# Attention phase: the next image's token sums made during the current image's output part, head sums ahead of four projection units, flows in another PSUM bank

## What is computed

```python
qkv = x @ W_qkv.T
q, k, v = (to_heads(part) for part in split(qkv))
q, k = sigmoid(q), sigmoid(k)
k_sum, q_sum = k.sum(axis=2), q.sum(axis=2)
sink_incoming   = 1 / (((q + EPS) * (k_sum + EPS)).sum(-1) + EPS)
source_outgoing = 1 / (((k + EPS) * (q_sum + EPS)).sum(-1) + EPS)
conserved_sink   = ((q + EPS) * ((k * source_outgoing).sum(2) + EPS)).sum(-1) + EPS
conserved_source = clip(((k + EPS) * ((q * sink_incoming).sum(2) + EPS)).sum(-1) + EPS, -1, 1)
kv  = einsum(k, v * softmax(conserved_source) * n)
out = einsum(q, kv) * sink_incoming * sigmoid(conserved_sink)
t   = t + out @ W_proj.T + b_proj
```

## Time and profile before

| | before |
|---|---|
| median of 3 executions | 5605.55 us (5603.51 to 5610.34) |
| profiled execution, its own time | 5614.06 us |
| its span in the profile | 5612.2 us |
| attention phase in the span | about 4040 to 5165 us |
| first head sums of image 0, of image 7 | start at 4094.8 us, at 5031.9 us |
| TensorE / VectorE / GpSimd busy over the span | 94% / 70% / 44% |
| mean granted TensorE clock over the span | 0.968 of full speed |

### The profile page before, as it was taken

The page is one execution under the profiler, slowest core; times in us unless marked ns, Lnnn a source line. Parts: engine busy times, 40 slices in busy tenths (PEclk is TensorE's granted clock), DMA queues, the critical chain, the costliest instruction groups (busy, mean ns, idle before and its releaser), DMA issues. The chain is left out here.

```text
span 5612.2 us, 90234 instructions
## 1 busy us (share of the span) xinstructions
PE 5297.2 (94%) x26964; PEld 3688.4 (66%) x26964; DVE 3942.1 (70%) x6109; ACT 2461.5 (44%) x4685; POOL 2495.2 (44%) x1385
## 2 busy tenths in 40 slices
PE   8999869998999999999998999999799999987999
PEld 5667545554555555555556777777676666665999
DVE  4555556665899999999995666676545555555787
ACT  4444238786334343443333555555532222210555
POOL 0000024442899999999995555555201111111332
PEclk9999879999999999999999999999899999997999
DMA  1111568887444444444446666666523333322443
GB/s 44 39 52 40 139 165 245 242 243 219 143 149 151 151 148 152 147 151 150 149 135 188 208 209 213 206 217 204 163 86 101 102 97 104 102 82 82 120 123 113
DMA packets 364270, 810.15 MB, mean 144 GB/s; under 512 B 45135, under 2 KB 149507, under 8 KB 354618
## 3 DMA queue, kind: packets, MB, share of 16 engines
q1 hardware_dynamic: 341648, 731.51, 44.3%
q10 hardware_dynamic: 22512, 77.20, 3.6%
HBM read 448.08 MB, written 360.49 MB: 144 GB/s over the span
## 5 line engine op out<-in xcount | busy, mean ns | idle before, releaser
L717 POOL TENSOR_TENSOR co_prod<-co_cross 111x512 f32<-111x512 f32 x448 | 850.2, 1898 | 0.0
L651 ACT ACTIVATE co_y_out<-co_y_ps 112x512 f32<-112x512 f32 x448 | 267.9, 598 | 927.6 <-PE co_y_ps L597 922.8
L714 POOL TENSOR_TENSOR co_prod<-co_direct 111x512 f32<-111x512 f32 x448 | 577.4, 1289 | 202.1 <-PE co_y_ps L597 115.4
L691 DVE TENSOR_TENSOR co_direct<-co_v_ps,co_spec 111x1024 f32<-111x1024 f32 x448 | 543.3, 1213 | 92.3 <-PE co_v_ps L135 87.8
L1917 POOL TENSOR_TENSOR at_t<-at_t,at_p_bias 112x1024 f32<-112x1024 f32 x56 | 134.2, 2409 | 976.1 <-DMA at_t<-t_tiles 976.1
L693 DVE TENSOR_TENSOR co_cross<-co_v_ps,co_spec 111x1024 f32<-111x1024 f32 x448 | 541.3, 1208 | 0.0
L135 PE MATMUL co_v_ps<-co_v_high,co_col_fwd_high 112*111 112x512 f32 x896 | 506.1, 565 | 1.4 <-DVE co_cross L693 1.4
L595 PE MATMUL co_y_ps<-co_prod,co_col_inv 111*112 111x512 f32 x896 | 458.2, 592 | 0.0
L597 PE MATMUL co_y_ps<-co_prod,co_col_inv 111*112 111x512 f32 x896 | 457.5, 592 | 0.1
L671 DVE TENSOR_TENSOR co_v_low<-co_v_in,co_v_high 112x1024 fp32r<-112x1024 f32 x224 | 372.4, 1662 | 0.1
L2081 ACT ACTIVATE at_qk_t<-at_bank_ps 128x448 f32<-128x448 f32 x224 | 121.8, 544 | 567.9 <-PE at_bank_ps L135 567.8
(11 more groups left out here) (267 smaller groups left out, 14107.8 us busy)
## 6 DMA issues: line engine op xcount, KB each, us to landing
v_rows<-pr_rows_out SPq DMA_DIRECT2D x56, 1792.0 KB
co_v_in<-v_rows SPq DMA_DIRECT2D x448, 224.0 KB
y_rows<-co_y_out SPq DMA_DIRECT2D x448, 224.0 KB
mx_y_in<-y_rows SPq DMA_DIRECT2D x224, 448.0 KB, 5.5
kern_rows<-kr_rows_out SPq DMA_DIRECT2D x28, 896.0 KB
st_x_in<-x SPq DMA_DIRECT2D x56, 448.0 KB, 11.4
pr_x_in<-x SPq DMA_DIRECT2D x112, 224.0 KB
mx_x_in<-x SPq DMA_DIRECT2D x56, 448.0 KB, 4.8
```

The source lines that it names most:

```text
L651: nc.scalar.activation(y_out[:, b, :], y_ps[b % 2][:2 * SIDE, :], ACT.Copy).then_inc(y_ready, 1)
L691: nc.vector.tensor_tensor(direct[b % 2][:], v_ps[b % 2][:POINTS, :], spec[i][:, :2 * WIDE], ALU.mult).then_inc(real_terms, 1)
L714: nc.gpsimd.tensor_tensor(prod[b % 2][:, :WIDE], direct[b % 2][:, :WIDE], direct[b % 2][:, WIDE:], ALU.subtract).then_inc(real_ready, 1)
L717: nc.gpsimd.tensor_tensor(prod[b % 2][:, WIDE:], cross[b % 2][:, :WIDE], cross[b % 2][:, WIDE:], ALU.add).then_inc(combined, 1)
```

## The change

VectorE: the token sums become a function `sum_tokens(im)`. For the first image it runs before the loop. For every other image it runs in the output part of the image before, at step j = 6, between `add_residual(5)` and `measure(5)`. TensorE: the head sums stand at the head of `back`, and units 0 to 3 stand behind them. The first flows go to bank 6 in place of bank 2. Before the gram part, `turn_keys(0)` and `turn_keys(1)` stand ahead of the `z` matmuls; unit 18 moves from before `add_gram(0)` to behind n = 1, and unit 19 from behind n = 4 to behind n = 5. The wait for `t2_ready` ahead of the first head sums stays. Nothing is added to or taken from the computation.

```diff
-        flow_ps = kept_ps = z_ps = kv_out_ps = bank[2]
+        flow_ps = bank[6]
+        kept_ps = z_ps = kv_out_ps = bank[2]
...
-                    units(0)
                     pe.wait_ge(t2_ready, b * SUMS)
                     pe.wait_ge(upd_ready, b * UPDS)
                     wait_link(pe, im, "sel")
                     head_sums(total_eps, flow_ps, flow_mm)
-                    units(1, 2, 3)
+                    units(0, 1, 2, 3)
                     wait_link(pe, im, "inv_low")
...
                     last.then_inc(turn_mm, 1)
+                    turn_keys(0)
+                    turn_keys(1)
                     for h in range(HALVES):
                         last = nc.tensor.matmul(z_ps[:, h:h + 1], z_rows[:, h, :], z_part[:], start=True, stop=True)
                     last.then_inc(z_mm, 1)
-                    turn_keys(0)
-                    turn_keys(1)
-                    units(18)
                     for n in range(NT):
                         add_gram(n)
                         if n + 2 < NT:
                             turn_keys(n + 2)
-                        if n == TILES:
-                            units(19)
+                        if n in (1, TILES + 1):
+                            units(18 + n // TILES)
...
+                def sum_tokens(im):
+
+                    dve.wait_ge(qt_ready, (im.b + 1) * UNITS)
                     step("total", nc.vector.reduce_sum(total[:], part[im.odd][:], axis=AX.X))
                     wait_link(dve, im, "total")
                     step("total_eps", nc.vector.tensor_scalar(total_eps[:], total[:], ATT_EPS, None, ALU.add))
                     wait_link(dve, im, "total_eps")
                     select("sel", total_eps)
...
                         if j:
                             add_residual(j - 1)
+                            if front and j == CHUNKS - 1:
+                                sum_tokens(ahead)
                             measure(j - 1)
...
                 low_part(first.after(), 1)
+                sum_tokens(first)
                 over_images(dve, back)
```

More of the change, by code:

```diff
@@ L2153, in low_part, with step, select @@
                     nc.vector.tensor_tensor(low[:], n_raw[im.slot(i)][:], high[:].bitcast(F32), ALU.subtract).then_inc(low_ready, 1)
+                def step(name, instruction):
+                    instruction.then_inc(link, 1)
+                mask3 = head_mask.unsqueeze(1).to_broadcast([128, 2, HB])
+                def select(name, sums):
+                    for x in (0, 2):
+                        y = (x + 2) % BLOCKS
+                        last = nc.vector.tensor_tensor(sel_heads[:, x:x + 2, :], mask3,
+                                                       sums[:, y:y + 2].unsqueeze(2).to_broadcast([128, 2, HB]), ALU.mult)
+                    step(name, last)
+                def sum_tokens(im):
+                    dve.wait_ge(qt_ready, (im.b + 1) * UNITS)
+                    step("total", nc.vector.reduce_sum(total[:], part[im.odd][:], axis=AX.X))
+                    wait_link(dve, im, "total")
+                    step("total_eps", nc.vector.tensor_scalar(total_eps[:], total[:], ATT_EPS, None, ALU.add))
+                    wait_link(dve, im, "total_eps")
+                    select("sel", total_eps)
                 def back(im, front, beyond):
@@ L2160, in next_low @@
                             low_part(ahead, i)
-                    def step(name, instruction):
-                        instruction.then_inc(link, 1)
                     def split_rows(name, values):
@@ L2169, in split_rows @@
                         step(name + "_low", nc.vector.tensor_tensor(rows[1][:], values[:], rows[0][:].bitcast(F32), ALU.subtract))
[L2171 to L2186, removed]
                     dve.wait_ge(const_mm, 2 * b + 1)
```

## The result

The changed kernel takes 5554.23 us (median of 4 executions, 5545.95 to 5566.60) against 5606.46 us before (4 executions): a ratio of 0.9914, 95% interval 0.9899 to 0.9929. The forecast was 5542 with a range of 5522 to 5575. The profiled execution took 5566.60 us, span 5564.8, the slowest of the four; the profiled execution of before (5614.06) was slower than all four that were timed with it, so the two profiles may be laid side by side.

A forecast was written before the change was run, and what follows sets the result against it. TensorE was taken as the bound over most of an image, its idle and half-clock time winnable. 19.3 + 18.2 + 3.4 + 8.4 + 10.8 + 3 + 0.5 = 63.6 us off 5605.55 gives 5542, range 5522 to 5575.

The forecast's parts named there:

- Head sums first: Image boundary, TensorE: head sums start 2.9 us earlier in images 1 to 6, 1.9 in image 7; 19.3 us.
- The token sums, moved forward: Output part, VectorE: four instructions, 0.7 us, fit its 0.81 us idle time; cost 0, at most 0.1 us per image.
- The chain leaves GpSimd behind: After the head sums: cast and subtraction finish before GpSimd's three additions, so their stretching goes; 18.2 us, ends 0 and 18.2.
- the clock of the head sums: Image boundary, TensorE: shorter idle time removes the low clock in two slow cases; 3.4 us, ends 0 and 3.4.
- The margin of 0.3 to 0.8 us: Room at two image boundaries between the chain's expected end and the start of GpSimd's additions.
- rival 1: After the head sums: GpSimd still catches the chain, losing 18.2 us and half the spread part's gain; 5564 us, chance 0.13.
- rival 2: Image boundary: clock low in all head sums, stretching remains; 23 us left of the gain, 5582 us, chance 0.08.
- The spread part: After the chain: TensorE at full clock saves 2.6 us, a stretched low part costs 1.2; 8.4 us, ends 1 and 16.
- The gram part: TensorE no longer waits for unit 18's sigmoid, continuing 1.5 us earlier in 7 images: 10.8 us, plus 3 for the clock.
- The term of the clock: Gram part: a shorter hole saves part of the low clock's cost; 3 us in all, ends 0 and 10.
- the poor end of 5555: The forecast's own slow end: without the gram clock, without image 0's gain, and with the low part fully stretched.

The follow-up runs named there:

- the gram half: The kernel before with only the changes ahead of and in the gram part (key transposes before the z matmuls, units 18 and 19 later): 5582.31 us, ratio 0.9970.

## Why the prediction held, and where it was wrong

**Head sums first** (19.3 us): measured 19.9. This step is right, to 0.1 us per image in images 1 to 6 and 0.2 in image 7, and so is its reason: with unit 0 back in its place the head sums still start 0.06 us behind the last addition, and the bank made no difference that shows. TensorE's idle time ahead of them is 2.2 to 2.5 us where it counted on 1.3, but that belongs to the next term: with the token sums one step earlier it is 0.8 to 1.0.

**The token sums, moved forward** is the step that failed: "the 0.7 us fit into that hole: cost 0, at most 0.1 us per image". Measured: 1.5 us per image, 10.6 in all. I had priced the four instructions at the place that they came from, where GpSimd is idle, and had not asked what GpSimd does where they go, although the row that gave me the hole said it: the hole ends on GpSimd's addition. One of the four waits that addition out: 1.95 to 2.31 us in place of 0.17 in all seven images. The bound was wrong too: not the 0.7 us of work but the 2.35 us of a GpSimd addition was the far end. Moving them one step earlier won the 1.5 us back, which shows the cause. The Trainium skill (SBUF — State Buffer, section Who interferes with whom) lists `tensor_scalar`, which this addition is, among the instructions that can contend with GpSimd, in the same section that I had used for the low part; the trace agrees, with 2.31 us against 0.17.

**The chain leaves GpSimd behind, and the clock of the head sums** (18.2 + 3.4, with 0.5 for image 0): measured 18.3. The sum comes near by its parts making up for each other. Less stretching gave 15.1 (cast and subtraction from 32.4 to 17.3 us). The term for the clock of the head sums, 3.4 us, came out at 0: a shorter hole was to keep the clock up, but the hole stayed at 2.2 to 2.5 us, and three of the eight head sums are at the low clock as before. Another 3.1 us, which I had not counted here, came from the first product: it starts 0.77 us behind the chain in place of 1.21 where TensorE begins the spread part at the full clock. The margin of 0.3 to 0.8 us that the sum relied on isn't there in images 1, 2 and 6 (two slow head sums; additions that start 10.0 us behind the last addition). That was rival 1 in one image and rival 2 in two.

**The spread part** (8.4 us): measured 1.2. The full clock gave 1.9 us each in images 1 and 2, whose low part was not stretched (and 0.6 in image 6, which had only 24.5 us before): 23.9 to 24.0 us in all three. The low part of chunk 2 took 2.0 to 3.2 us in images 3 to 5, within the ends that I gave it, but I had left out what it sets off: TensorE waits for the products behind it, the clock falls, and 1 to 2 us become up to 5.6. With the biases held back all of it is gone, in every image.

**The gram part** (10.8 + 3 us): measured 21.2. The hole was priced right: image 1, at the full clock before and after, gained 1.3 us. The term of the clock was mis-sized, 3 us where it gave some 10: the gram part takes 35.1 to 35.5 us in every image now, where it took 35.6 to 39.6. That is the good end that I had given this term, and not what I expected.

**The rest.** The attention phase gained 50.1 us where the sum said 63.6: 10.6 less by the token sums, 7.2 by the spread part and 3.8 by the chain, 7.4 more by the gram part and 0.6 by the boundary. That the time came as near as 12 us to the forecast is in part luck: a third of what the three terms lost was made up by the gram part's clock. The terms are sums over one execution; the median of the runs moved by 52 us and the profiled executions by 47.5, as the changed kernel reaches its first head sums 2.6 us later. Two slips of arithmetic decide nothing: the poor end of 5555 is 5553 by its own terms, and the chances add up to 0.99.

## What to carry to other kernels

A VectorE instruction's price belongs to its place: before moving even a 0.17 us one, look at what GpSimd runs there, since either may have to wait for the end of the other's instruction (0.17 us became up to 2.31). When a profile shows such stretching, the first question is whether GpSimd's work is needed now; here moving that alone was worth 36 us. And a wait of 2 us on TensorE costs more than 2 us when the clock is low behind it (the head sums then take 1.4 to 1.7 us longer): price a hole with what follows it.

## What the runs showed that I had not expected

- A VectorE addition on 128 x 4 numbers took up to 2.31 us in place of 0.17, since it ends with GpSimd's 2.35 us addition; a reduction (0.17 us), the statistics (1.41 for four) and the products with one input from PSUM (0.62) were not slowed beside GpSimd.
- After idle stretches of TensorE of up to 1.2 us none of 34 head sums showed the low clock; after 2.2 to 3.0 us 29 of 57 did (means of 0.77 to 0.80 over the head sums).
- Two halves of a change gave 0.30% and 0.20% alone and 0.86% together. Each half alone leaves a hole behind which the clock is often low, but the excess is close to the scatter of the next point, so it isn't shown. Why the low clock met six images in a row in the gram half is open.
- Kernels whose images meet GpSimd by tenths of a microsecond seem to scatter more than an interval from 4 or 5 runs says: two that differ in a bank alone gave 0.9914 and 0.9944 in different series, and 0.9862 and 0.9860 once GpSimd's additions were out of the way.
